# A decoder layer on one core: layer-norm statistics taken elsewhere and in pieces, fourteen copies on another engine

## The reference

```python
x = x + attn(layernorm(x), q_w, q_b, k_w, k_b, v_w, v_b, o_w, o_b)   # causal softmax attention
x = x + xattn(layernorm(x), ctx, ctx)                               # the same, no projections
x = x + ffn(layernorm(x))

def layernorm(x):                       # over the 512 columns
    return (x - mean(x)) / sqrt(var(x) + 1e-5)
def ffn(x):
    rw = softmax(top_2(x @ W_gate.T))   # 8 experts
    return relu(x @ W_up.T) @ W_down.T + sum(rw) * (x @ W_expert)
```

## Time and profile before

| | |
|---|---|
| Median of 3 runs | 714.7 us (713.9 to 716.91) |
| Profiled execution | 711.97 us |
| its span, first to last instruction | 710.0 us |
| busy: PE, ACT, DVE, POOL | 674.7, 501.4, 494.6, 256.9 us |
| mean granted clock of PE | 0.995 of full speed |

### The profile page before, as it was taken

The page is one execution under the profiler, slowest core; times in us unless marked ns, Lnnn a source line. Parts: engine busy times, 40 slices in busy tenths (PEclk is TensorE's granted clock), DMA queues, the critical chain, the costliest instruction groups (busy, mean ns, idle before and its releaser), DMA issues.

```text
span 710.0 us, 13884 instructions
## 1 busy us (share of the span) xinstructions
PE 674.7 (95%) x4488; PEld 523.8 (74%) x4488; DVE 494.6 (70%) x1730; ACT 501.4 (71%) x1450; POOL 256.9 (36%) x391
## 2 busy tenths in 40 slices
PE   7998999999999999999889987999989999899998
PEld 6777777777787777777666755777768777677786
DVE  6568766766766776776878788767887669664632
ACT  5678877777876778787899887776588667874110
POOL 4745644333555335742564415333112102000100
PEclk9999999999999999999999999999999999999999
DMA  9763533336423573445946584633463443510101
GB/s 313 186 155 75 141 70 90 82 94 185 116 61 90 124 212 84 102 105 146 275 122 168 153 236 121 166 95 97 96 183 89 111 101 87 163 38 1 59 1 59
DMA packets 52327, 86.12 MB, mean 121 GB/s; under 512 B 8609, under 2 KB 16801, under 8 KB 52257
## 3 DMA queue, kind: packets, MB, share of 16 engines
q1 hardware_dynamic: 52256, 85.25, 46.1%
HBM read 27.55 MB, written 7.34 MB: 49 GB/s over the span
## 4 chain that ended last, share of the span: by engine, by line
PE 80%; DVE 7%; ACT 6%; issue 2%; DMA 2%; POOL 2%; SPq 1%; POOLq 0%; ACTq 0%; DVEq 0%
PE t L480 16%; PE m L519 14%; PE m L520 14%; PE m L521 14%; PE pv L513 9%; PE s L466 8%; DVE probs L682 3%; ACT probs L910 3%; ACT prob L919 1%; PE m L585 1%; DVE prob L692 1%; DMA stack<-stage 1%; POOL probs L1023 1%; PE m L480 1%; PE m L534 1%
## 5 line engine op out<-in xcount | busy, mean ns | idle before, releaser
L682 DVE CUSTOM_DVE_ANT_0 probs<-s,mask 128x128 f32<-128x128 f32 (+3 forms) x512 | 246.6, 483 | 130.7 <-PE s L466 129.0
L910 ACT ACTIVATE probs<-probs,negmax 128x128 f32<-128x128 f32 (+3 forms) x512 | 284.5, 559 | 46.1 <-DVE negmax L682 45.2
L480 PE MATMUL t<-ident,probs 128*128 128x128 f32 x1140 | 203.5, 277 | 11.4 <-ACT prob L919 6.5
L466 PE MATMUL s<-stack 96*128 96x128 f32 (+3 forms) x512 | 197.8, 394 | 5.5 <-DVE negmax L682 2.8
L1023 POOL TENSOR_SCALAR probs<-probs,rsum 128x128 f32<-128x128 f32 (+3 forms) x256 | 133.4, 539 | 176.9 <-DVE rsum L696 176.6
L919 ACT ACTIVATE prob<-t 128x384 f32<-128x384 f32 (+1 forms) x231 | 124.7, 540 | 97.7 <-PE t L480 96.7
L480 PEld LDWEIGHTS t<-ident,probs 128*128 128x128 f32 x1140 | 144.7, 141 | 60.6 <-ACT prob L919 10.5
L466 PEld LDWEIGHTS s<-stack 96*128 96x128 f32 x512 | 97.9, 191 | 18.7 <-DVE negmax L682 4.1
L910 ACT ACTIVATION_READ_ACCUMULATOR probs<-probs,negmax 128x1 f32 x512 | 98.9, 193 | 0.0
L692 DVE COPY prob<-t 128x256 f32<-128x256 f32 (+1 forms) x218 | 77.1, 354 | 30.9 <-PE t L480 29.9
L519 PE MATMUL m<-xT_hi,w_lo 128*128 128x512 f32 x192 | 78.3, 408 | 1.2 <-DVE xT_lo L750 1.2
(11 more groups left out here) (144 smaller groups left out, 946.2 us busy)
## 6 DMA issues: line engine op xcount, KB each, us to landing
stack<-stage SPq DMA_DIRECT2D x384, 128.0 KB, 2.3
xt<-in_x SPq DMA_DIRECT2D x16, 256.0 KB, 4.7
xres<-in_x SPq DMA_DIRECT2D x4, 1024.0 KB, 6.1
kraw<-in_ctxT SPq DMA_DIRECT2D x16, 256.0 KB, 3.0
cv<-in_ctx SPq DMA_DIRECT2D x16, 256.0 KB, 3.1
x<-xres SPq DMA_DIRECT2D x3, 1024.0 KB, 5.5
...
```

The source lines that it names most:

```text
L466: nc.tensor.matmul(score_tile(P, i), stack[0:RS, P % 2, h, 0, chunk(qb)], stack[0:RS, P % 2, h, 1, 0:N], start=True, stop=True).then_inc(s ...
L480: mm = nc.tensor.transpose(dst[:, chunk(qb - kb)], probs[:, (2 * P + h) % 3, OFF[qb] + PART * kb:OFF[qb] + PART * kb + PART], ident[:, :])
L682: nc.vector.tensor_tensor_reduce(probs[:, (2 * P + h) % 3, OFF[qb]:OFF[qb + 1]], score_tile(P, i), mask[:, T - N:T], -SCALE, BIG, ALU.add, ...
L910: nc.scalar.activation(tile, tile, ACT.Exp, bias=negmax[:, P % 2, h, qb:qb + 1], scale=-1.0, accum_out=total).then_inc(p_exp, 1)
```

## The change

**Cross statistics.** For batches 0 to 2 they are taken from `xres` right behind the output projection (`c_stats_of`), one slot behind the emptying of each of its four tiles: steps 10, 11, 11, 12 (batch 0), 18, 19, 19, 20 (batch 1), 25, 28, 29, 30 (batch 2). The reload is waited for by the norm alone. POOL's scale moves with them, to steps 12, 20 and 30. SP waits for them before it loads the next batch's residual over `xres`. Batch 3 keeps step 48.

**FFN statistics.** They go by cross group: the four tiles of the 128 columns that `added(G)` has just written, at slots 1, 2, 4 and 5 of step 2G + 3 (31, 35, 39, 41, 43 and so on to 65). Each waits for c_out of that group. The aggregation stands in the steps of the last group of a batch, 41, 49, 57 and 65, as before, and takes four pieces in one instruction.

**Copies.** In pairs 28 to 41 (LIGHT) DVE copies the transposed tile 1 (384 columns) in place of ACT, 14 copies.

**FFN transposes.** The four of batches 0 to 2 (jobs FL, in steps 43, 51 and 59) stand at slots 1, 2, 5, 6 in place of 1, 2, 4, 5.

**Start.** The first transposes go to other banks, and the twelve matmuls of the first query and key groups stand in another order: the products of high parts first, then those with the low parts, in the order in which these are made.

```diff
@@ schedule
+LIGHT = range(2 * CROSS_AT[0], PAIRS * (B + 1) + 2)
+def act_turns(P):
+    return (0, 4, 5) if P in LIGHT else T_ACT
+def dve_turns(P):
+    return tuple(i for i in range(PAIRS) if i not in act_turns(P))
...
-def stats_slots(j):
-    z = PAIRS * PAIRS * (j - 1)
-    if j <= B:
-        z -= 2 * PAIRS if j == B else 0
-        return [z - 8, z - 7, z, z + 1]
-    if j == B + 2:
-        return [z + 19, z + 20, z + 21, z + 22]
-    return [z, z, z + 16, z + 16] if j == B + 1 else [z, z, z + 1, z + 1]
+def o_start(b, t):
+    if b == B - 1:
+        return PAIRS * (SELF_END + min(t, 2)) + 4 * (t // 3)
+    if b == B - 2:
+        return PAIRS * (25, 28, 29, 29)[t] + 4 * (t // 3)
+    return PAIRS * (PAIRS * (b + 1) + 1 + t) + (4, 4, 0, 1)[t]
+def stats_slots(b):
+    z = PAIRS * PAIRS * (b - 1)
+    return [z - 8, z - 7, z, z + 1]
+def c_stats_slots(b):
+    z = PAIRS * PAIRS * (2 * B - 2)
+    return [z, z, z + 1, z + 1] if b == B - 1 else [o_start(b, t) + NT + 1 for t in range(NT)]
...
-def f_stats_slots(f):
-    z = PAIRS * (PAIRS * (f + B + 1) + 1)
+def f_stats_slots(G):
+    z = PAIRS * (2 * G + 3)
     return [z + 1, z + 2, z + 4, z + 5]
...
-                put(("FL", f, m), 0, u + 1 + m + m // 2, 1, 1)
+                put(("FL", f, m), 0, u + 1 + m + 2 * (m // 2), 1, 1)
...
-        first_bank = [*m_bank, pv_bank, t_bank[0]]
+        first_bank = [*s_bank, pv_bank]
@@ SP, before the residual of the next batch is loaded
                     sp.wait_ge(x2_stored[b - 1], 16)
+                    sp.wait_ge(c_mv_done, NT * b)
                     sp.dma_start(xres[:, :, :], x_in[b]).then_inc(res_loaded, 16)
@@ PE, the first group of queries (w == WQ) and of keys
+            def first_three(dst, w, k):
+                late = ([("lo", c) for c in (0, 1)] + [("x", c) for c in range(KC)] + [("lo", c) for c in (2, 3)] if w == WQ else
+                        [("x", c) for c in range(KC)] + [("lo", c) for c in range(KC)])
+                terms = [("hi", c) for c in range(KC)] + late
...
@@ DVE
-            def f_stats_of(f, t):
-                if t == 0:
-                    dve.wait_ge(c_out, KC * (f + 1))
-                nc.vector.bn_stats(f_stats[:, t, :], RES[f][:, t, :]).then_inc(f_stat, 1)
-                dve.wait_ge(f_stat, NT * f + t + 1)
-                nc.vector.bn_aggr(f_mv[:, t, :], f_stats[:, t, :]).then_inc(f_mv_done, 1)
+            def c_stats_of(b, t):
+                dve.wait_ge(o_out, NT * b + t + 1)
+                nc.vector.bn_stats(c_stats[:, t, :], xres[:, t, :]).then_inc(c_stat, 1)
+                dve.wait_ge(c_stat, NT * b + t + 1)
+                nc.vector.bn_aggr(c_mv[:, b, t, :], c_stats[:, t, :]).then_inc(c_mv_done, 1)
+            def f_stats_of(G, t):
+                n = RANK[G]
+                f = n // KC
+                dve.wait_ge(c_out, n + 1)
+                nc.vector.bn_stats(f_stats[:, t, n % KC, :], RES[f][:, t, chunk(n % KC)]).then_inc(f_stat, 1)
+                if n % KC == KC - 1:
+                    dve.wait_ge(f_stat, NT * n + t + 1)
+                    nc.vector.bn_aggr(f_mv[:, t, :], f_stats[:, t, :, :].rearrange("p c s -> p (c s)")).then_inc(f_mv_done, 1)
...
-                    if 0 <= s < NP and i in T_DVE:
+                    if 0 <= s < NP and i in dve_turns(s):
                         turned(s, i)
                     if own(s // 2) and i == 1:
                         recip(s, 1)
@@ ACT
-                    if 0 <= s < NP and i in T_ACT:
+                    if 0 <= s < NP and i in act_turns(s):
                         turned(s, i)
@@ POOL, step s, behind the scalings and added(G)
+                for j in range(B):
+                    if s == c_stats_slots(j)[-1] // PAIRS:
+                        c_scale(j)
                 for f in range(B):
-                    if s == f_stats_slots(f)[-1] // PAIRS:
+                    if s == f_stats_slots(CROSS_AT[KC * f + KC - 1])[-1] // PAIRS:
                         f_scale(f)
```

More of the change, by code:

```diff
@@ L87, in other @@
     return 0 <= G < NG and not IS_SELF[G]
+LIGHT = range(2 * CROSS_AT[0], PAIRS * (B + 1) + 2)
[3 more added lines that the diff above has]
+    return tuple(i for i in range(PAIRS) if i not in act_turns(P))
+ACT_TURNS = [sum(len(act_turns(p)) for p in range(P)) for P in range(NP)]
 def own_rank(P):
@@ L273, in decoder_block @@
         rstd = sb("rstd", [PART, NT])
-        f_stats = sb("f_stats", [PART, NT, 6])
+        c_stats = sb("c_stats", [PART, NT, 6])
+        c_mv = sb("c_mv", [PART, B, NT, 2])
+        c_veps = sb("c_veps", [PART, B, NT])
+        c_rstd = sb("c_rstd", [PART, B, NT])
+        f_stats = sb("f_stats", [PART, NT, KC, 6])
         f_mv = sb("f_mv", [PART, NT, 2])
@@ L521, in three @@
                 return nc.tensor.matmul(dst, lhs[0], rhs[0], start=False, stop=(c == KC - 1))
+            def first_three(dst, w, k):
+                late = ([("lo", c) for c in (0, 1)] + [("x", c) for c in range(KC)] + [("lo", c) for c in (2, 3)] if w == WQ else
+                        [("x", c) for c in range(KC)] + [("lo", c) for c in range(KC)])
+                terms = [("hi", c) for c in range(KC)] + late
+                for n in range(3 * k, 3 * k + 3):
+                    term, c = terms[n]
+                    if term == "hi":
+                        pe.wait_ge(w_hi_done[w], c + 1)
+                        pe.wait_ge(lnt_hi, c + 1)
+                    elif term == "x":
+                        pe.wait_ge(lnt_lo, c + 1)
+                    elif w == WQ and c >= 2:
+                        pe.wait_ge(wq_rest, c - 1)
+                    else:
+                        pe.wait_ge(w_lo_done[w], c + 1)
+                    weight = w_lo if term == "lo" else w_hi
+                    mm = nc.tensor.matmul(dst, weight[:, w, c, chunk(0)], (xT_lo if term == "x" else xT_hi)[:, c, :],
+                                          start=(n == 0), stop=(n == 3 * KC - 1))
+                return mm
             def bank_for(key):
@@ L549, in fill @@
                     w = WQ if kind == "Q" else WK
-                    if n == 0 and kind == "Q" and c >= 2:
-                        pe.wait_ge(wq_rest, c - 1)
-                    elif n == 0:
-                        pe.wait_ge(w_lo_done[w], c + 1)
-                    if kind == "Q" and n % KC == 0:
-                        pe.wait_ge(lnt_lo, KC * (n // KC) + c + 1)
-                    mm = three(dst, (w_hi[:, w, c, chunk(n % KC)], w_lo[:, w, c, chunk(n % KC)]),
-                               (xT_hi[:, c, :], xT_lo[:, c, :]), c)
+                    if kind == "Q" and n and n % KC == 0:
+                        pe.wait_ge(lnt_lo, KC * (n // KC) + c + 1)
+                    if n == 0:
+                        mm = first_three(dst, w, c)
+                    else:
+                        mm = three(dst, (w_hi[:, w, c, chunk(n % KC)], w_lo[:, w, c, chunk(n % KC)]),
+                                   (xT_hi[:, c, :], xT_lo[:, c, :]), c)
                     if c == KC - 1:
@@ L883, in _ @@
                         back_scaled(s // 2 - 1)
-                    for j in range(1, 2 * B):
+                    for j in range(1, B):
                         for t in range(NT):
@@ L887, in _ @@
                                 ln_stats(j, t)
+                    for j in range(B):
+                        for t in range(NT):
+                            if z == c_stats_slots(j)[t]:
+                                c_stats_of(j, t)
+                    for j in range(1, 2 * B):
                         for t in range(NT):
                             if z == norm_slots(j)[t]:
-                                ln_norm(j, t)
+                                ln_norm(j, t) if j < B else c_norm(j - B, t)
+                    for G in CROSS_AT:
+                        for t in range(NT):
+                            if z == f_stats_slots(G)[t]:
+                                f_stats_of(G, t)
                     for f in range(B):
-                        for t in range(NT):
-                            if z == f_stats_slots(f)[t]:
-                                f_stats_of(f, t)
                         for t in range(NT):
@@ L916, in turned @@
                 act.wait_ge(t_mm, PAIRS * P + i + 1)
-                if P % 2 == 0 and h == 0:
+                if P % 2 == 0 and (h == 0 or i - NT not in act_turns(P)):
                     need(act, pv_done, NT * (P // 2 - 1) + kb + 1)
```

60 lines of the change are left out of this document (30 added, 30 removed).

## The result

The changed kernel takes 729.04 us (727.52 to 730.74), the kernel before beside it 715.17: a ratio of 1.0193, interval 1.0157 to 1.0229. It is 14 us slower, where 1.8 were forecast and 720.5 was the end of the range. The profiled execution has a span of 725.9 us.

The account below looks back on a forecast made before the run. PE, busy 674.7 of 710.0 us, was taken as the bound, with DVE full in steps 41 and 42. Terms -5.8 + 2.9 + 3.4 + 0.5 + 0.8 = +1.8 us, put on the 714.7 median: 716.5; range 710.0 to 720.5.

Parts of the forecast that it names:

- Both of its signs of being wrong on the slow side: Steps 31 to 37 over 59.5 us (nothing given back), or additional stretches at clock 0.50 (the clock falls).
- The second pair of FFN transposes moves one slot later: Steps 51 and 59: PE's 1.5 us wait for a low part of DVE shortens, -0.8 us for both (0 to -1.0).
- The two stalls: Steps 31 and 35: DVE's statistics wait 3.4 us for POOL's residual sum; +2.9 and +3.4 us, at most 4.35 each.
- what is given back I price by ACT: Steps 31 to 37: stall time recovered, priced by ACT losing a 0.48 us copy per pair; leaves +2.9 and +3.4 us.
- Rival (b): Nothing is given back at steps 31 and 35, as PE, ACT and DVE wait for each other: +4.2, 718.9 us; chance 0.17.
- It is there before DVE asks: From step 39 on, cross groups have no scalings ahead of POOL's residual sum, so DVE need not wait for it.
- rival (c): The clock falls: stalls in steps 31 and 35 add two half-clock stretches, 1.7 us of lost work each: 719.9 us; chance 0.11.
- a half clock that would go in step 43: Step 43: half clock worth 1.7 us of PE work goes, against four new statistics; term -1.0 us (0 to -2.3).
- ACT with 7.33 is next: Step 42: DVE falls to 6.5 us, ACT's 7.33 is next; step lasts 7.9, -2.3 us (-1.2 to -2.9).
- rival (d): The relief isn't there: ACT or PE holds steps 41 to 43 up at once: +2.8, 719.3 us; chance 0.07.
- full cover for 28 and half for the others: Moved cross statistics: +0.8 us for steps 11 and 19 (0 to 1.7), 0 for others; 0.86 each without cover.
- The -0.3 of the start: Start: PE's 1.2 us wait for a low part that the new order asks for later; -0.3 us (0 to -1.2).

Follow-up runs that it names:

- the fast version: Changed kernel with old copies and FFN transpose slots, moved statistics of batches' inner parts at slot 0 of even steps: 708.4 us, 0.9916 of the kernel before.
- the slope of the runs: 61 runs of the unchanged kernel before, beside the experiments, differing in mean granted clock: 0.45 us for each 0.001 of mean clock.

## Why the prediction was wrong

The forecast, the range and the side were wrong: it forecast no difference, with 0.35 on slower. Both of its signs of being wrong on the slow side came: steps 31 to 37 over 59.5 us, and more stretches at 0.50. The terms, after less before, from the steps of the two profiled executions:

| places | term | measured |
|---|---|---|
| start | -0.3 | -0.3 |
| steps 11 to 13 and 19 to 21 | +0.8 | +1.4 |
| steps 24 to 30 | +0.5 | +1.6 |
| steps 31 to 33 | +2.9 | +4.3 |
| steps 34 to 37 | +3.4 | +4.9 |
| steps 40 and 41 | -1.4 | -1.3 |
| step 42 | -2.3 | 0.0 |
| step 43 | -1.0 | -0.8 |
| steps 44 to 50 | 0 | +3.1 |
| steps 51 to 61 | -0.8 | +3.2 |
| sum of the span | +1.8 | +15.9 |

**FL, the step with the wrong sign.** "The second pair of FFN transposes moves one slot later" was read as 0.8 us less wait. The working looked at the wait that shortens and not at who reads the last low part: the gate projection, at slot 0 of the next step. The last transpose moved from slot 5 to 6, so that read now waits about 2 us in steps 44, 52 and 60. The question "where a stall goes, what is late next" was not put here. At full clock steps 59 and 60 lose 0.8 together (-0.6 and +1.4), where the term had them gain 0.4. Alone, the slots cost 0.35%, in the fast version 0.5%. In the changed kernel steps 44 to 61 hold 6.3 us, 3.3 of them the half clock in 44 and 52; taking the slots back removes some 0.4% of the time.

**The two stalls: mechanism and length right, the price wrong.** The stall was forecast as 3.4 us twice, and the reciprocal 0.95 later; the rows show 3.43 and 3.42, and the run with the reciprocal ahead 0.93. What failed is "what is given back I price by ACT". ACT's relief in step 33 came (8.15 to 7.10), but the copies themselves cost as much in the steps around it, as their run alone shows, so ACT paid for nothing. Rival (b), "nothing is given back", has the size, 8.7 us for a measured 9.2, but in part by luck: at full clock a wait of 3.4 cost 2.8, so some of it is absorbed, and the half clock behind each stall, which (b) did not have, came on top. Moving the statistics behind the sum took 8 us away again. "It is there before DVE asks", said of the sum from step 39 on, failed in step 43, where DVE waits 2.1 us.

**The clock: rival (c), with 0.11.** The prediction counted a half clock that would go in step 43, and left the ones that new waits would bring to a rival. In the trace five stretches at 0.50 stand where two stood, each behind a wait that had not been there or had been shorter. The Trainium skill ("TensorE: Matmul & The Clock Gate", section "HAM oscillation") says that waits between bursts of matmuls bring the lower clock; the trace agrees with its five stretches, though not every such wait brought one (step 60). Their share is an estimated 3.8 us by the slope of the runs, and more by the places. A wait of 2 us on PE had to be priced with the 1.6 that a stretch behind it costs.

**Step 42: not DVE's for long.** "ACT with 7.33 is next" held only where the clock stayed up: 7.2 to 8.2 us in four traces, for a forecast of 7.9. In the changed kernel PE awaits the transfer of the next queries for 2.0 us just ahead of it, and the values run at half clock. The view that the earlier trace rows is taken from had this transfer before the change, and the prediction left its row out:

```profile
PE s L466 <- DMA stack<-stage: 1.0, 1, 1.0
```

For this step that was rival (d) in effect, by another cause: DMA and clock, not ACT or PE. What makes the transfer late stays open. It isn't the shorter step 41 alone: PE waits 0.6 and 0.9 us with the copies back and with the reciprocal ahead, where step 41 takes 6.90 and 7.19, and 1.7 with the FL slots alone, where it takes 8.12 as before.

**Smaller steps.** The cross statistics cost 0.7 to 0.8 at each of steps 11, 19 and 28, where the prediction had full cover for 28 and half for the others. The 0.7 of step 30 come with the copies: it takes 11.08 with the moved statistics and no copies, 11.70 with the copies alone. One set of statistics stands in it, not the two that the prediction counted. By its own run the cross part gains 0.45% all the same. The -0.3 of the start is not shown: it moves between -0.5 and +1.0 in the traces that have the new start. The piece of 128 columns took 286 ns (0.28 estimated), the copy of 384 555 ns (0.56). Four pieces in place of 512 columns thus add 4 x 0.286 - 0.676 = 0.47 us; by the formula that the prediction took from the Trainium skill ("VectorE: DVE Perf Modes", "The TRN2 errata") it would have been 0.2. The same section adds that this formula gives too little for a single operation, and that the fixed term measured is about 150 cycles, not 58. With 150 the estimate is 0.47, and the trace agrees. The load was not what cost the time. The part on step 43, where the wait was to be small because the weight splits start earlier, was right in direction: 2.1 us in the change, 5.2 where the cross statistics stay.
